# Cross attention with fp32 layer norm, one core: last pass's norm on GpSimd, range check between the output norms, epsilon as bias of the root, an early read of the choice

## The reference

```python
Q = (input_Q @ W_Q).reshape(b, -1, N_HEADS, D_K).transpose(0, 2, 1, 3)
K = (input_K @ W_K).reshape(b, -1, N_HEADS, D_K).transpose(0, 2, 1, 3)
V = (input_V @ W_V).reshape(b, -1, N_HEADS, D_V).transpose(0, 2, 1, 3)
scores = jnp.einsum('bhqd,bhkd->bhqk', Q, K) / np.sqrt(D_K)
attn = jax.nn.softmax(scores, axis=-1)
context = jnp.einsum('bhqk,bhkd->bhqd', attn, V)
out = context.transpose(0, 2, 1, 3).reshape(b, -1, N_HEADS * D_V) @ W_O + input_Q
mu = jnp.mean(out, axis=-1, keepdims=True)
var = jnp.var(out, axis=-1, keepdims=True)
return (out - mu) / jnp.sqrt(var + 1e-05)
```

## Time and profile before

| | us |
|---|---|
| median of 3 runs | 1595.1 (1595.03 to 1595.64) |
| the profiled execution, its own time | 1594.82 |
| its span, first to last instruction | 1593.0 |
| TensorE busy (matmuls) | 1584.1, 99% of the span |
| VectorE busy | 1344.2, 84% |
| ScalarE busy | 928.6, 58% |
| GpSimd busy | 284.6, 18% |

### The profile page before, as it was taken

How to read it: one execution, slowest core, us unless ns; L and a number is a source line. 1 busy time by engine, 2 the same in 40 slices (tenths; PEclk the granted TensorE clock), 3 DMA queues, 4 the chain that set the end, 5 groups by cost and what they waited for, 6 DMA issues and landing times.

```text
span 1593.0 us, 43935 instructions
## 1 busy us (share of the span) xinstructions
PE 1584.1 (99%) x19164; PEld 982.0 (62%) x19164; DVE 1344.2 (84%) x1397; ACT 928.6 (58%) x1080; POOL 284.6 (18%) x313
## 2 busy tenths in 40 slices
PE   9999999999999999999999999999999999999998
PEld 4576666666665556666666666666666666666435
DVE  7888798887888879888798878988789887898877
ACT  4345566556655556655566556565566655665553
POOL 3561012120121201202012021120211102111000
PEclk9999999999999999999999999999999999999999
DMA  6321011000110001101011010110011100120000
GB/s 214 95 73 34 12 31 59 12 31 11 42 59 2 31 21 38 53 2 31 21 49 42 2 31 22 59 32 2 30 32 51 30 2 30 32 60 22 9 1 15
DMA packets 31618, 56.68 MB, mean 36 GB/s; under 512 B 7120, under 2 KB 13392, under 8 KB 31424
## 3 DMA queue, kind: packets, MB, share of 16 engines
q1 hardware_dynamic: 31136, 53.51, 10.9%
q10 hardware_dynamic: 288, 0.33, 0.1%
HBM read 48.02 MB, written 5.30 MB: 33 GB/s over the span
## 4 chain that ended last, share of the span: by engine, by line
PE 98%; DVE 1%; issue 0%; ACT 0%; DVEq 0%; ACTq 0%
PE s_ps L664 43%; PE o_ps L681 43%; PE w_ps L730 5%; PE w_ps L747 2%; PE w_ps L761 1%; PE w_ps L766 1%; PE w_ps L782 1%; PE w_ps L783 1%; PE w_ps L762 1%; PE w_ps L779 0%; PE w_ps L768 0%; DVE sums L1117 0%; PE s_ps L859 0%; DVE inv_sum L1227 0%; DVE y L1260 0%
## 5 line engine op out<-in xcount | busy, mean ns | idle before, releaser
L978 ACT ACTIVATE probs<-s_ps 128x1024 f32<-128x1024 f32 x801 | 819.7, 1023 | 619.4 <-PE s_ps L664 615.6
L1117 DVE TENSOR_TENSOR sums<-sums,probs 128x1024 f32<-128x1024 f32 x785 | 984.7, 1254 | 123.3 <-ACT probs L978 90.0
L681 PE MATMUL o_ps<-probs,v_all 64*64 64x512 f32 x6408 | 919.6, 589 | 0.0
L664 PE MATMUL s_ps<-q_sb,k_all 64*64 64x512 f32 x6408 | 918.0, 589 | 0.0
L681 PEld LDWEIGHTS o_ps<-probs,v_all 64*64 64x64 f32 x6408 | 388.4, 133 | 241.7 <-issue 120.3
L664 PEld LDWEIGHTS s_ps<-q_sb,k_all 64*64 64x64 f32 x6408 | 380.3, 133 | 221.3 <-issue 106.4
L616 POOL TENSOR_TENSOR crossed<-crossed 128x128 f32<-128x128 f32 x84 | 41.8, 497 | 719.2 <-ACT crossed L996 719.2
L1074 DVE TENSOR_REDUCE v_all<-w_ps 128x512 f32<-128x1024 f32 (+2 forms) x103 | 122.0, 1184 | 40.0 <-PE w_ps L730 39.7
L730 PEld LDWEIGHTS w_ps<-wv_sb,ctx_all 64*64 64x64 f32 x3176 | 108.1, 133 | 45.3 <-issue 18.6
L730 PE MATMUL w_ps<-wv_sb,ctx_all 64*64 64x128 f32 x3176 | 115.8, 269 | 0.3 <-DVE y L1142 0.3
L994 ACT ACTIVATE crossed<-w_ps 64x384 f32<-64x384 f32 x168 | 81.5, 485 | 16.7 <-PE w_ps L768 14.5
(11 more groups left out here) (115 smaller groups left out, 670.9 us busy)
## 6 DMA issues: line engine op xcount, KB each, us to landing
c_forms<-forms_dram SPq DMA_DIRECT2D x84, 384.0 KB, 3.1
forms_dram<-c_forms SPq DMA_DIRECT2D x12, 384.0 KB, 2.5
inv_sum<-inv_dram SPq DMA_DIRECT2D x30, 128.0 KB, 2.9
attn<-in_ctxT SPq DMA_DIRECT2D x24, 128.0 KB, 2.9
ctx_all<-in_ctxT SPq DMA_DIRECT2D x11, 256.0 KB, 5.4
quad_rows<-quad_sums SPq DMA_DIRECT2D x60, 4.0 KB, 1.8
c_forms<-in_ctxT SPq DMA_DIRECT2D x12, 64.0 KB, 2.5
x_sb<-in_x SPq DMA_DIRECT2D x1, 512.0 KB, 9.6
```

The costliest lines, as they stand in the source:

```text
L664: last = nc.tensor.matmul(s_ps[part(half), u % 2, head * QH:(head + 1) * QH], k_all[part(head), c * P + half * DH:c * P + (half + 1) * DH] ...
L681: last = nc.tensor.matmul(o_ps[part(head), rows, :], v_all[part(rows), key_chunk(t, c, head), part(head)], probs[part(rows), u % RING, hea ...
L978: nc.scalar.activation(probs[:, u % RING, :], s_ps[:, u % 2, :], ACT.Exp, scale=SCALE).then_inc(probs_ready, 1)
L1117: nc.vector.tensor_tensor(out=sums[0:rows, t % 2, :], in0=sums[0:rows, t % 2, :], in1=probs[0:rows, u % RING, :], op=ALU.add).then_inc(sum ...
```

## The change

On VectorE the last pass's norm goes, and a reciprocal of one column (`limits` of `key_totals`) stands in its place; GpSimd does the norm, as the last instruction of its program. `layer_norm` loses the addition of epsilon; ScalarE's root reads the variance with epsilon as bias, and VectorE takes the reciprocal of the root. The range reductions over `inv_sum` go; ScalarE makes a copy of `sums` with a running sum before the root's table is loaded and a copy of `inv_sum` with a running sum behind it. The check on `extremes` moves from behind group (2,3) to behind group (0,1), the count's product from behind tile 6 to behind tile 4, `use_general` from behind group (4,5) to behind group (2,3), and VectorE loads it there. In pass 0, "sl" goes from step 23 to 25, "vw" from 25 to 27, the exponential from 27 to 29, and SyncE's load of the rows one block back.

```diff
-    LEFT_STEP, LEFT_EXP_STEP = 40, 27
-    LEFT_WORK = {15: "kl", 17: "vl", 19: "wt", 21: "gl", 23: "sl", 25: "vw"}
+    LEFT_STEP, LEFT_EXP_STEP = 40, 29
+    LEFT_WORK = {15: "kl", 17: "vl", 19: "wt", 21: "gl", 25: "sl", 27: "vw"}
...
-    LEFT_BEHIND = 7
+    LEFT_BEHIND = 8
...
# GpSimd
+            pool.wait_ge(o_added, PASSES)
+            pool.wait_ge(inv_ready, 1)
+            nc.gpsimd.tensor_tensor(out=attn[:, PAIRS - 1, QH:NQ], in0=o_a[:, :], in1=inv_sum[:, :],
+                                    op=ALU.mult).then_inc(last_norm_done, 1)
...
# TensorE
             project_output(4, [PAIRS - 1]).then_inc(y_done, 1)
-            project_output(5, range(PAIRS)).then_inc(y_done, 1)
-
-            pe.wait_ge(work_ready, READY["d", PASSES - 1, 0])
-            project_output(6, range(PAIRS)).then_inc(y_done, 1)
-
             pe.wait_ge(y_taken, 2)
             pe.wait_ge(exact_ready, 1)
             nc.tensor.matmul(s_ps[0:1, 0, 0:1], exact[:, :], ones[:, 0:1], start=True, stop=True).then_inc(exact_counted, 1)
+            project_output(5, range(PAIRS)).then_inc(y_done, 1)
+
+            pe.wait_ge(work_ready, READY["d", PASSES - 1, 0])
+            project_output(6, range(PAIRS)).then_inc(y_done, 1)
             project_output(7, range(PAIRS)).then_inc(y_done, 1)
...
# ScalarE
-                    act.wait_ge(inv_var_ready, len(GROUPS) * turn + n + 1)
+                    act.wait_ge(ln_step, steps_before(turn, n + 1))
                     ts = slice(tiles[0], tiles[-1] + 1)
-                    nc.scalar.activation(rstd[:, ts], inv_var[:, ts], ACT.Sqrt).then_inc(rstd_ready, 1)
+                    nc.scalar.activation(rstd[:, ts], mean_var[:, ts, 1], ACT.Sqrt, bias=eps[:, 0:1]).then_inc(std_ready, 1)
...
+            act.wait_ge(sums_done, UNITS)
+            act.wait_ge(pv_done, UNITS)
+            nc.scalar.activation(probs[:, 0, :], sums[:, (PASSES - 1) % 2, :], ACT.Copy, scale=float(P),
+                                 accum_out=key_totals[:, 0:1]).then_inc(totals_ready, 1)
             act.wait_ge(consts_ready, 2)
             nc.scalar.activation(rstd[:, 0:1], ones[:, 0:1], ACT.Sqrt).then_inc(table_loaded, 1)
+            act.wait_ge(inv_ready, 1)
+            act.wait_ge(limits_set, 1)
+            nc.scalar.activation(probs[:, 1, 0:QH], inv_sum[:, :], ACT.Copy,
+                                 accum_out=limits[:, 0, PASSES - 1:PASSES]).then_inc(limits_done, 1)
...
# VectorE
             nc.vector.reciprocal(inv_sum[:, :], inv_sum[:, :]).then_inc(inv_ready, 1)
-            dve.wait_ge(o_added, PASSES)
-            dve.wait_ge(inv_ready, 1)
-            nc.vector.tensor_tensor(out=attn[:, PAIRS - 1, QH:NQ], in0=o_a[:, :], in1=inv_sum[:, :],
-                                    op=ALU.mult).then_inc(last_norm_done, 1)
+            dve.wait_ge(totals_ready, 1)
+            nc.vector.reciprocal(limits[:, 1, last:PASSES], key_totals[:, :]).then_inc(limits_done, 1)
...
-                    dve.wait_ge(ln_step, before + 2 * len(tiles))
                     ts = slice(tiles[0], tiles[-1] + 1)
-                    nc.vector.tensor_scalar(out=inv_var[:, ts], in0=mean_var[:, ts, 1], scalar1=EPS, scalar2=None,
-                                            op0=ALU.add).then_inc(ln_step, 1)
-                    dve.wait_ge(ln_step, before + 2 * len(tiles) + 1)
-                    nc.vector.reciprocal(inv_var[:, ts], inv_var[:, ts]).then_inc(inv_var_ready, 1)
+                    dve.wait_ge(std_ready, len(GROUPS) * turn + n + 1)
+                    nc.vector.reciprocal(rstd[:, ts], rstd[:, ts]).then_inc(rstd_ready, 1)
...
-            layer_norm(0, (0, 1))
-
-            for n in range(2):
-                nc.vector.tensor_reduce(out=limits[:, n, last:PASSES], in_=inv_sum[:, :], axis=AX.X,
-                                        op=(ALU.add, ALU.min)[n]).then_inc(limits_done, 1)
+            layer_norm(0, (0,))
...
-            layer_norm(0, (2,))
+            layer_norm(0, (1,))
...
+            chosen = load_choice(dve)
...
-            layer_norm(0, (3, 4))
+            layer_norm(0, (2, 3, 4))
...
-            if_general(dve, load_choice(dve), general_and_norm)
+            if_general(dve, chosen, general_and_norm)
```

More of the change, by code:

```diff
@@ L187, in cross_attention_kernel @@
         mean_var = sb("mean_var", [P, QT, 2])
-        inv_var = sb("inv_var", [P, QT])
+        eps = sb("eps", [P, 1])
+        key_totals = sb("key_totals", [P, 1])
         rstd = sb("rstd", [P, QT])
@@ L273, in cross_attention_kernel @@
         table_loaded = sem("table_loaded")
-        inv_var_ready = sem("inv_var_ready")
+        eps_set = sem("eps_set")
+        totals_ready = sem("totals_ready")
+        std_ready = sem("std_ready")
         rstd_ready = sem("rstd_ready")
@@ L394, in g_nothing, with steps_before @@
             pass
+        def steps_before(turn, n):
+            return sum(2 * len(group) for group in GROUPS * turn + GROUPS[:n])
         def load_choice(eng):
@@ L900, in _ @@
             project_output(4, [PAIRS - 1]).then_inc(y_done, 1)
+            pe.wait_ge(y_taken, 2)
+            pe.wait_ge(exact_ready, 1)
+            nc.tensor.matmul(s_ps[0:1, 0, 0:1], exact[:, :], ones[:, 0:1], start=True, stop=True).then_inc(exact_counted, 1)
             project_output(5, range(PAIRS)).then_inc(y_done, 1)
@@ L904, in _ @@
             project_output(6, range(PAIRS)).then_inc(y_done, 1)
-            pe.wait_ge(y_taken, 2)
-            pe.wait_ge(exact_ready, 1)
-            nc.tensor.matmul(s_ps[0:1, 0, 0:1], exact[:, :], ones[:, 0:1], start=True, stop=True).then_inc(exact_counted, 1)
             project_output(7, range(PAIRS)).then_inc(y_done, 1)
@@ L1058, in general_and_roots @@
                 roots(1)
+            act.wait_ge(sums_done, UNITS)
+            act.wait_ge(pv_done, UNITS)
+            nc.scalar.activation(probs[:, 0, :], sums[:, (PASSES - 1) % 2, :], ACT.Copy, scale=float(P),
+                                 accum_out=key_totals[:, 0:1]).then_inc(totals_ready, 1)
             act.wait_ge(consts_ready, 2)
             nc.scalar.activation(rstd[:, 0:1], ones[:, 0:1], ACT.Sqrt).then_inc(table_loaded, 1)
+            act.wait_ge(inv_ready, 1)
+            act.wait_ge(limits_set, 1)
+            nc.scalar.activation(probs[:, 1, 0:QH], inv_sum[:, :], ACT.Copy,
+                                 accum_out=limits[:, 0, PASSES - 1:PASSES]).then_inc(limits_done, 1)
             act.wait_ge(table_loaded, 1)
+            act.wait_ge(eps_set, 1)
             roots(0)
@@ L1070, in _ @@
             nc.vector.memset(limits[:, :, :], 1.0).then_inc(limits_set, 1)
+            nc.vector.memset(eps[:, :], EPS).then_inc(eps_set, 1)
             dve.wait_ge(limits_set, 1)
@@ L1237, in layer_norm @@
                     tiles = GROUPS[n]
-                    before = sum(2 * len(g) + 1 for g in GROUPS * turn + GROUPS[:n])
+                    before = steps_before(turn, n)
                     for t in tiles:
```

## The result

| | before | this |
|---|---|---|
| median of 22 runs each, us | 1595.17 (1594.34 to 1596.07) | 1592.38 (1591.76 to 1593.70) |
| the profiled execution, its own time | 1594.82 | 1592.52 |
| its span | 1593.0 | 1590.7 |
| first row of the product of sums with ones, the start of "the tail" here | 1570.12 | 1570.04 |
| the tail, from that row to the span's end | 22.88 | 20.66 |

The ratio is 0.9983, 95% interval 0.9977 to 0.9989: 2.8 us, clear of no change but within the 0.2% taken as the bound. The forecast was 1593.1 us and a gain of 2.0.

The account below looks back on a forecast made before the run. TensorE, 99% busy, bounds the loop and a VectorE chain the end; VectorE saves 0.41 + 1.0 + 1.31 - 0.9 = 1.8 us, TensorE bounds from tile 7, and a 2.0 us gain gives 1593.1 us, range 1592.3 to 1594.8.

Parts of the forecast that it names:

- Norm to GpSimd: Last pass's norm: GpSimd takes 1.27 us, covered by tiles 0 to 4; VectorE's group 0 starts 0.41 us sooner.
- the rival in which GpSimd holds the adds: VectorE's output adds wait for GpSimd's norm until 1578.16; only 0.7 us won, 1594.4 us; chance 0.10.
- Epsilon as bias: Layer norm in the tail: one small VectorE operation a group goes, 5 x 0.20 = 1.0 us off VectorE.
- I add nothing: ScalarE's root: no row shows a bias read's cost, so the root is kept at 0.20 us.
- Range check: Tail: two reductions, 1.31 us, leave VectorE for ScalarE copies with running sums, in time for group 0's root.
- Check, count and choice earlier: Tail: check done 1.1 us before TensorE's count; VectorE's 0.9 us load before group 2 mostly covered by tile 5.
- TensorE as the bound: From tile 7, at 1586.00, VectorE's group 4 waits for TensorE; last norm over 1.5 us sooner.
- The end: Behind the last norm: VectorE drains at 1590.3, SyncE at 1590.4; end between 1590.7 and 1591.1, gain 2.0 us.
- TensorE is next: At the end: TensorE's branch at 1586.6 lasts 4142 ns, so it drains after 1590.8; could be earlier, not later.
- the rival in which the branches disturb each other: Refetches and last stores coincide at 1587 to 1590; TensorE drains at 1592.0, time 1594.3 us; chance 0.12.
- Pass 0: Left-over keys' pieces two steps later, the load of rows one block later: costs nothing, 0.3 us either way.
- the slower side: Slower by over 0.2%, by a moved pass 0 piece late for TensorE: 5.2 us, 1598.5 us or more; chance 0.04.

Follow-up runs that it names:

- twice the work: The changed kernel with GpSimd's last norm made twice, first into a buffer nothing reads: 1592.97 us, tail 21.20 us.
- load at the end: The changed kernel with VectorE's load of the choice back behind its last norm: 1593.43 us, tail 21.40 us.
- both profiles of the one before: The kernel before the change, profiled a second time unchanged: 1594.82 and 1595.15 us, tails 22.88 and 22.84 us.
- the kernel with the range check: The changed kernel with the two range reductions back on VectorE and without ScalarE's two copies: 1594.93 us, tail 22.29 us.
- the kernel with order and early load alone: The changed kernel with norm, range check and epsilon back on VectorE, keeping the new order and early load: 1594.63 us, tail 23.26 us.
- the two kernels with 60 more instructions: 60 one-column memsets added to VectorE's last pass, in the changed kernel (1592.99 us) and in that with VectorE's load at its end (1592.38 us).
- 147: 147 one-column memsets added likewise, in the changed kernel (1592.38 us) and in that with VectorE's load at its end (1594.12 us).

## Why the prediction was right, and where not

The time, the side and the bound of 0.2% were right: 1592.4 against 1593.1, within the range but only 0.1 us above its lower end, 1592.3; the gain is 2.8 us where 2.0 was forecast. That most steps came near and that the misses below nearly cancel is in part luck. By its steps:

- **Norm to GpSimd.** The GpSimd row is the 1.27 us taken. Group 0 starts 0.77 us sooner into the tail (6.62 to 5.85), forecast 0.41. The term was mis-sized twice by 0.18: I charged VectorE's small reciprocal the 0.20 spacing of its kind, but the add starts 0.02 us behind it; and I let it start where the norm had, 0.10 us behind the big reciprocal, but it starts 0.08 ahead of that one's end. Nothing was held, by the margin of 0.25 us shown above; the rival in which GpSimd holds the adds is refuted by their 0.47 us. The Trainium skill's rule, to which I gave 0.2 us only for a slow GpSimd, is real at this place: 0.7 us on the norm with twice the work.
- **Epsilon as bias.** 0.10 us a group, not 0.20: the operation goes, but the root takes 0.30 us instead of 0.20. The step "I add nothing" failed; over five groups 0.5 us instead of 1.0.
- **Range check.** 1.31 us off VectorE; ScalarE's copies with their sums ended at 1576.72, 0.4 us before the first root, as argued. Its running sum costs 0.20.
- **Check, count and choice earlier.** The count found its input ready. VectorE's hole is 1.0 us (forecast 0.9), the wait for tile 5 comes, and neither costs the last norm anything (load at the end: 17.72 in both).
- **TensorE as the bound.** Not quite: group 4's add was to wait for TensorE and did not. VectorE comes 0.1 us behind it, at the pace of its own chain. The group starts add up: -0.77 at group 0, +0.49 to group 1 (check in, epsilon out), -0.94 to group 2 (reductions and check out, load in), +0.03, -0.07 and -0.11 for the rest, together the 1.37 us by which the last norm comes sooner. The forecast was 1.5; the two mis-sized terms, 0.36 and 0.5, cancel nearly, and the wait for tile 5 takes the rest.
- **The end.** Here a step failed, without changing the time: "TensorE is next", at 1590.8, "it could come earlier". It did. Its load had been waiting for the choice until 1585.7 and was at 1583.8 now, so its drain came at 1588.8. Its branch lasted 4.12 us against 4.14, so the rival in which the branches disturb each other has nothing for it. VectorE's drain ended the span as before, at 1590.5, where I had put 1590.3. I had written that I would be wrong if the end stayed at VectorE's drain; it stayed, and two of my ends (VectorE 1590.3, SyncE 1590.4) lay so near that the sum held.
- **Pass 0** is worth nothing that the runs can show, as costed.
- **Slips of arithmetic:** the slower side begins at 1598.3 us and not 1598.5, and 5.2 us is seventeen times the wait seen, not sixteen. Nothing hangs on either.

The sum in one profile each: 2.22 us in the tail, 0.08 ahead of it. What lies ahead hides two opposite things. The first score matmul of the changed kernel started 0.3 us later in that execution, as it varies; and from the copy of pass 0 to that of the last pass TensorE took 1446.24 to 1446.29 us in all changed kernels against 1446.51 and 1446.52 in both profiles of the one before. So the kernel gained 0.25 us inside the loop as well, which I had not forecast. It is in the fifth pass (103.39 and 103.38 us before, 103.09 after). In both profiles of the kernel before, VectorE stands idle there for 0.46 us with nothing that it waits for, in a stretch where it is tight, and TensorE is late behind it. The two timelines, before and after:

```profile
420.01 1.23 DVE L1117 TENSOR_TENSOR sums<-sums,probs 128x1024 f32<-128x1024 f32 x1 [0.46 <-DVE sums L1117]
```

```profile
418.49 2.55 DVE L1138 TENSOR_TENSOR sums<-sums,probs 128x1024 f32<-128x1024 f32 x2
```

In the changed kernels such idle times of 0.46 us stand elsewhere (the first at 326.39 us), and cost less. Each of them ends 0.7 us ahead of a packet of instructions of 8 KB on q14: at 420.68 us before, at 327.07, 497.42 and 591.17 with the change, where idle times end at 420.01, 326.39, 496.76 and 590.46. So they stand where VectorE goes from one block of instructions to the next, and the memset that sets `eps` moves all of VectorE's later instructions one place on against these borders. That this one place is the 0.25 us was not tried; the layout of memory differs too.

Tail 2.2 and loop 0.25 make some 2.5 us of the 2.8 between the medians. The rest is less than the start-up and pass 0 vary by (1.5 and 0.5 us across these profiles).

**What is left open:** why the gap in the kernel with the range check was 3.7 us instead of 3.0 (ScalarE's own packet of instructions on q14 starts within 0.2 us of VectorE's there, but it does within 0.3 us in the kernel with order and early load alone too, whose gap is 3.1); why the last store takes between 1.8 and 3.8 us. It was longer where a transfer of instructions (queue q8 of the profile) fell into its first half, as with the load at the end, and no run separates the two.

## What to carry to other kernels

An operation taken off the engine that ends a kernel is worth its start-to-start distance up to the next thing that is waited for, here tile 5, tile 7 and the last store, and no more: write down the next bounds before adding up savings. Reordering alone can lose; check that what is pulled forward is ready where it is now asked for (the count: 0.92 us of waiting without the savings, none with them). And in the last microseconds read the sequencers' rows: a branch behind the last instruction can cost more than any operation in front of it, and how much depends on where it stands in the stream.

## What the runs showed of the hardware that I had not expected

- A branch of VectorE that is taken was followed by 2.8 to 3.7 us of nothing in twelve profiles, with a packet of instructions 1.0 us behind the branch, and by 0.6 us without one in the two kernels with 60 more instructions ahead of it; 147 brought it back. TensorE's branch lasted 3.4 to 4.2 us. ScalarE's drain followed its branch by less than 0.2 us; behind SyncE's stands a wait, so its cost is not seen.
- VectorE's instructions came in packets of 8 KB, one per 128 rows, TensorE's in packets of 16 KB. Where VectorE was tight, going from one to the next cost it 0.46 us of idle time.
- Loading one register from SBUF blocked VectorE's queue for 1.0 us: 0.54 for the load, 0.21 and 0.04 for the rows behind it, and the rest around them.
- An activation with a per-partition bias took 0.30 us on 128x2 and 0.29 on 128x1, without one 0.20 on either; a running sum adds a row of 0.19 to 0.20 us of its own.
- Even a `tensor_scalar` of 128x2 waits for GpSimd (0.17 to 0.39 us), while adds with one input in PSUM do not (0.47 us for two, as without GpSimd).
